# Three quarters of a fused LayerNorm and linear layer by Strassen's seven products, on eight cores

## The chip, the cores and the metric

The kernel runs on the eight cores of one Trainium2 chip. Each core works on 1024 of the 8192 tokens and shares nothing with the others. The metric is the device time of the slowest core in microseconds; lower is better.

## The reference

With `x` of 8192 tokens x 4096 features, `W` of 4096 outputs x 4096 inputs and a bias per output:

```python
def _layernorm(x, axis=-1, eps=1e-5):
    m = jnp.mean(x, axis=axis, keepdims=True)
    v = jnp.var(x, axis=axis, keepdims=True)
    return (x - m) / jnp.sqrt(v + eps)

x = L0_attn_x                                   # (1, 8192, 4096)
x = x + _L0_attn_ref(_layernorm(x))             # softmax over one key: it returns 2 * its input
x = x + _L0_ffn_ref(_layernorm(x), ...)         # y = LN(x) @ (aa * tanh(kk * W)).T + bias
```

The attention has a batch of one, so its softmax is over a single score and is one; its output is twice the normalized input. What is left is two layer norms in a row, which fold into one scale and one offset per token, a large matrix product, and a residual that is again x with one scale and offset per token, plus the bias.

## The kernel before

Each core has 1024 tokens as eight tiles of 128 (`NT`), 4096 inputs as 32 blocks of 128, and 4096 outputs as eight columns of 512 (`NO`). The work has two parts.

In the first part x comes tile by tile. VectorE computes the statistics and from them the coefficients of the token (`statistics`, `coefficients`); ScalarE and GpSimd normalize chunks of 1024 inputs into `h2b` (L384, L242); TensorE transposes them (L424), and ScalarE copies the transposed chunks from PSUM into `h2T` (L391), which holds all 1024 tokens, inputs on the partitions, in bf16. Meanwhile W arrives in pieces of 512 KB (128 inputs x 2 blocks x 512 outputs, f32) in a ring of four buffers `wr`; SP loads piece w as soon as ScalarE has done piece w-4 (`load_w`), and ScalarE writes tanh(kk * W) in bf16 into `wp` (L376). `wp` has two buffers of 16 pieces, one column of 512 outputs each.

The product is made in groups: one group is a token tile and a column of outputs, 32 matmuls (16 pieces, two each) that accumulate in one PSUM bank (L439). The tokens are the stationary operand and W the moving one. The order is written out in `tensor_order()`: column 0 is interleaved with the arrival of tiles, then the first five tiles of column 1 go through together, piece by piece, and from there on the groups follow each other, column by column. `closed` lists the groups in the order in which they end, and `bank_of` and `bank_free` give each a bank and the eviction that it waits for (`NBANK` is six; two banks serve the transposes).

VectorE evicts group i in two instructions (`evict`): L345 makes the residual, rb * s1 + bias, and after a drain L353 adds the PSUM bank to it and writes `outs`. GpSimd serves group i (`serve`): it waits for the eviction, stores `outs` (L262) and loads the residual of group i+4 (L254), all in one queue and in this order. `load_bias` brings the bias of a column, broadcast over the partitions. The last eight groups are stored by SP.

Of the kernel before, what the change touches and what calls it, by code (L numbers as in the profile page):

```python
# [17 lines left out]
D = 4096  # L18
TOK = 1024
NT = TOK // 128  # L20
NO = D // 512
# [5 lines left out]
NBANK = 6  # L27
NRB = 4
# [16 lines left out]
JOIN = [0, 3, 6, 9, 12, 15]  # L45

# [46 lines left out]
def build_nc():  # L93
# [3 lines left out]
    w_h = nc.dram_tensor("wpieces", [NO * PPB * 128, PW], F32, kind="ExternalInput")  # L97
    br_h = nc.dram_tensor("biasrow", [1, D], F32, kind="ExternalInput")
# [3 lines left out]
    y_h = nc.dram_tensor("y", [TOK, D], F32, kind="ExternalOutput")  # L102
# [20 lines left out]
    sc = sb("sc", [128, 8], F32)  # L123

# [6 lines left out]
    acc = [es.enter_context(nc.psum_tensor(f"acc{i}", [128, 512], F32)) for i in range(NBANK)]  # L131
    ptr = [es.enter_context(nc.psum_tensor(f"ptr{i}", [128, CW], BF16)) for i in range(2)]
# [21 lines left out]
    s_ev = sem("s_ev")  # L154

# [13 lines left out]
    NG = len(closed)  # L169

# [19 lines left out]
    @block.sync  # L190
    def _(sync):
        def load_x(t):
            for c in range(NCH):
                if t in before:
                    wait_normalized(sync, before[t], c)
                sync.dma_start(x_of[t][:, c * CW:(c + 1) * CW],  # L196
                               x_h[t * 128:(t + 1) * 128, c * CW:(c + 1) * CW]).then_inc(s_x[t % 4][c], 16)

        def load_w(w):
            if w >= RING:  # L200
                sync.wait_ge(s_wt, w - RING + 1)
# [24 lines left out]
        for i in range(NG - NT, NG):
            t, ot = closed[i]
            sync.wait_ge(s_ev, i + 1)
            sync.dma_start(y_h[t * 128:(t + 1) * 128, ot * 512:(ot + 1) * 512],
                           outs[i % NRB][:, :]).then_inc(s_z[i % NRB], 16)  # L230
        for i in range(NRB):
            sync.wait_ge(s_y[i], 16 * ((NG - NT) // NRB))
            sync.wait_ge(s_z[i], 16 * (NT // NRB))

    @block.gpsimd
    def _(gpsimd):
# [38 lines left out]
        for i in range(EVICTED, NG):  # L275
            serve(i)

    @block.vector
    def _(vector):
# [54 lines left out]
        def evict(i):  # L334
# [110 lines left out]

    es.close()
# [35 lines left out]
```

## Time and profile before

| | us |
|---|---|
| median of 3 runs (lowest to highest) | 522.54 (520.4 to 523.31) |
| the profiled execution, device time | 519.82 |
| its span, slowest core | 518.3 |
| spans of the eight cores | 513.1 to 518.3 |
| mean granted TensorE clock of the cores | 0.965 to 0.979 |

Rows of the trace are of the slowest core, in microseconds from the start of its span. Busy time of an engine is the time in which it executes; its idle time before an instruction is put down to what released it. Matmuls are pipelined, so their busy times overlap, and a few records can be missing; spacings between evictions are the safer clock.

### The profile page before, as it was taken

The numbers are of one execution on the slowest core, as the hardware profiler recorded it, in microseconds if no ns is written. First come the engines' busy times: TensorE is split into PE (matmuls) and PEld (weight loads), VectorE is DVE, ScalarE is ACT, GpSimd is POOL, SyncE is SP. The second block draws the span as 40 slices with busy tenths as digits, with TensorE's granted clock in tenths as the row PEclk, the third lists the DMA queues.
The fourth block names the chain that finished last, engine by engine and source line by source line (L and its number), as shares of the span: only waits on it lengthen the run. The fifth ranks groups of instructions, "written<-read, shape, count | busy, mean of one in ns | idle before, by whom it ended". The sixth has DMA issues, their size and how long they took to land.

```text
span 518.3 us, 6903 instructions; the slowest of 8 cores (513.1 to 518.3 us)
## 1 busy us (share of the span) xinstructions
PE 475.9 (92%) x2364; PEld 225.4 (43%) x2364; DVE 161.1 (31%) x337; ACT 194.8 (38%) x177; POOL 87.3 (17%) x142
## 2 busy tenths in 40 slices
PE   0676879869999999999999999999999999999996
PEld 0543345435444444444444444444444444444442
DVE  1776585883003322222112222221122222211221
ACT  0496756675466244414350324314430435000000
POOL 0111111443003121111111211111111211110000
PEclk9857989989999999999999999999999999999999
DMA  6999999879999999965995399828993696222211
GB/s 169 301 287 316 299 301 272 316 238 264 306 279 255 317 329 330 302 237 165 274 338 218 78 265 291 319 83 249 306 308 132 140 300 270 81 82 81 83 40 41
DMA packets 35282, 120.02 MB, mean 232 GB/s; under 512 B 5168, under 2 KB 5168, under 8 KB 35248
## 3 DMA queue, kind: packets, MB, share of 16 engines
q1 hardware_dynamic: 25056, 87.57, 53.2%
q0 software_dynamic: 9760, 31.99, 20.9%
q8 instruction: 19, 0.31, 0.2%
q14 instruction: 15, 0.12, 0.2%
q10 hardware_dynamic: 432, 0.03, 0.1%
HBM read 102.79 MB, written 16.78 MB: 231 GB/s over the span
## 4 chain that ended last, share of the span: by engine, by line
PE 77%; DMA 12%; DVE 4%; SPq 2%; issue 1%; DVEq 1%; ACT 1%; ACTq 0%
PE acc L439 77%; DMA xs<-x 7%; DMA wr<-wpieces 6%; SPq L196 2%; DVE stats L298 1%; PE ptr L424 1%; ACT h2b L384 0%; ACT wp L376 0%; DVEq L299 0%; SPq L202 0%; DVE sc L288 0%; DVE sc L284 0%; DVEq L347 0%; DVE mv L300 0%; DVE sc L290 0%
## 5 line engine op out<-in xcount | busy, mean ns | idle before, releaser
L439 PE MATMUL acc<-wp,h2T 128*128 128x512 bf16 x2048 | 452.5, 382 | 6.1 <-ACT wp L376 6.0
L439 PEld LDWEIGHTS acc<-wp,h2T 128*128 128x128 bf16 x2048 | 200.2, 98 | 246.2 <-issue 12.5
L376 ACT ACTIVATE wp<-wr,kk_sb 128x1024 bf16<-128x1024 f32 x128 | 144.5, 1146 | 202.1 <-DMA wr<-wpieces 130.8
L353 DVE SCALAR_TENSOR_TENSOR outs<-acc,b1a,rb 128x512 f32<-128x512 f32 x64 | 48.1, 751 | 299.2 <-PE acc L439 296.8
L262 POOL DMA_DIRECT2D y<-outs x56 | 30.7, 548 | 282.7 <-DVE outs L353 282.3
L345 DVE SCALAR_TENSOR_TENSOR rb<-rb,s1a,bb 128x512 f32<-128x512 f32 x64 | 47.6, 744 | 17.1 <-DMA rb<-x 16.6
L424 PE MATMUL ptr<-ident_sb,h2b 128*128 128x128 bf16 x256 | 23.8, 257 | 17.6 <-ACT h2b L384 17.2
L254 POOL DMA_DIRECT2D rb<-x x60 | 32.8, 546 | 27.3 <-DVE outs L353 24.9
L298 DVE BATCH_NORM_STATS2 stats<-xs 128x6 f32<-128x512 f32 x48 | 29.8, 681 | 20.4 <-DMA xs<-x 20.0
L391 ACT COPY h2T<-ptr 128x1024 bf16<-128x1024 bf16 x32 | 31.1, 1011 | 11.9 <-PE ptr L424 11.8
L424 PEld LDWEIGHTS ptr<-ident_sb,h2b 128*128 128x128 bf16 x256 | 20.5, 118 | 27.5 <-issue 25.6
L242 POOL TENSOR_SCALAR h2b<-xs,cf 128x1024 bf16<-128x1024 f32 x12 | 16.2, 1360 | 69.5 <-DVE cf L325 69.5
L413 PE MATMUL acc<-ident_sb 128*128 128x128 bf16 x60 | 5.8, 289 | 14.5 <-DMA aa_sb<-aa 14.5
L384 ACT ACTIVATE h2b<-xs,cf 128x1024 bf16<-128x1024 f32 x12 | 14.2, 1232 | 11.7 <-DVE cf L325 11.7
L413 PEld LDWEIGHTS acc<-ident_sb 128*128 128x128 bf16 x60 | 5.7, 135 | 14.4 <-issue 14.4
L298 DVE BATCH_NORM_STATS2 stats<-h2T 128x6 f32<-128x512 f32 x16 | 10.2, 685 | 4.7 <-DMA h2T<-x 4.5
L242 POOL TENSOR_SCALAR h2b<-h2T,cf 128x1024 bf16<-128x1024 f32 x4 | 4.7, 1195 | 21.1 <-DVE cf L325 21.1
L376 ACT ACT_TABLE_LOAD x1 | 1.3, 1283 | 16.8 <-DMA wr<-wpieces 16.8
L284 DVE TENSOR_SCALAR sc<-sc 128x1 f32<-128x1 f32 x16 | 4.4, 273 | 1.3
L288 DVE TENSOR_SCALAR sc<-sc 128x1 f32<-128x1 f32 x16 | 4.4, 273 | 1.3
L384 ACT ACTIVATE h2b<-h2T,cf 128x1024 bf16<-128x1024 f32 x4 | 4.7, 1226 | 0.0
L248 POOL DMA_DIRECT2D bb<-biasrow x6 | 3.3, 546 | 0.0
(16 smaller groups left out, 22.5 us busy)
## 6 DMA issues: line engine op xcount, KB each, us to landing
wr<-wpieces SPq DMA_DIRECT2D x128, 512.0 KB, 8.8
rb<-x POOLq DMA_DIRECT2D x60, 256.0 KB, 7.2
y<-outs POOLq DMA_DIRECT2D x56, 256.0 KB, 6.0
xs<-x SPq DMA_DIRECT2D x24, 512.0 KB, 13.7
h2T<-x SPq DMA_DIRECT2D x8, 512.0 KB, 18.8
y<-outs SPq DMA_DIRECT2D x8, 256.0 KB, 2.0
bb<-biasrow POOLq DMA_DIRECT2D x6, 256.0 KB, 11.1
rb<-x SPq DMA_DIRECT2D x4, 256.0 KB, 11.4
```

The costliest lines, as they stand in the source:

```text
L242: gpsimd.tensor_scalar(h2b[:, c * CW:(c + 1) * CW], x_of[t][:, c * CW:(c + 1) * CW], cf[t % 2][:, 0:1], cf[t % 2][:, 1:2], ALU.mult, ALU.a ...
L254: gpsimd.dma_start(rb[i % NRB][:, :], x_h[t * 128:(t + 1) * 128, ot * 512:(ot + 1) * 512]).then_inc(s_rb[i % NRB], 16)
L262: gpsimd.dma_start(y_h[t * 128:(t + 1) * 128, ot * 512:(ot + 1) * 512], outs[i % NRB][:, :]).then_inc(s_y[i % NRB], 16)
L298: vector.bn_stats(stats[:, 6 * k:6 * k + 6], x_of[t][:, 512 * k:512 * (k + 1)])
L345: vector.scalar_tensor_tensor(r[:, :], r[:, :], s1a[:, t:t + 1], bb[ot % 2][:, :], ALU.mult, ALU.add)
L353: vector.scalar_tensor_tensor(o[:, :], acc[bank_of[t, ot]][:, :], b1a[:, t:t + 1], r[:, :], ALU.add, ALU.add).then_inc(s_ev, 1)
L376: scalar.activation(wp[ot % 2][:, p * PW:(p + 1) * PW], wr[w % RING][:, :], AF.Tanh, bias=0.0, scale=kk[:, :]).then_inc(s_wt, 1)
L384: scalar.activation(h2b[:, c * CW:(c + 1) * CW], x_of[t][:, c * CW:(c + 1) * CW], AF.Identity, bias=cf[t % 2][:, 1:2], scale=cf[t % 2][:, ...
L391: scalar.copy(h2T[:, t * D + c * CW:t * D + (c + 1) * CW], ptr[c % 2][:, :]).then_inc(s_eA, 1)
L413: tensor.matmul(acc[0][:, 0:128], ident[:, :], ident[:, :], start=True, stop=True)
L424: mm = tensor.transpose(ptr[i % 2][:, q * 128:(q + 1) * 128], h2b[:, c * CW + q * 128:c * CW + (q + 1) * 128], ident[:, :])
L439: mm = tensor.matmul(acc[bank_of[t, ot]][:, :], h2T[:, t * D + k * 128:t * D + (k + 1) * 128], wp[ot % 2][:, k * 512:(k + 1) * 512], start ...
```

## The change

The first 1024 outputs are made as before (`NO` is now 2: 16 groups). The other 3072 are made in 12 pairs (`NP`) of two blocks of 128 outputs by Strassen's method, in which a 2 x 2 block product takes seven block products instead of eight. The halves of A are tokens (512 each) x inputs (2048 each); the halves of B are inputs x the two output blocks of the pair. The result is made transposed: W is now stationary, 128 outputs wide, and the tokens are the moving operand, four tiles of 128 columns at once. A product is 16 matmuls in one bank, and all eight banks take part once the transposes are over.

Sums of quarters of A are made once by VectorE, in bf16, on 128x2048 at a time, four for each of five sums: sA5, sA2 and sA1 in regions that x and `wp` had used, A12-A22 and A21-A11 in place in `h2T`. Sums of W (S6, D12, S7, D21, S1) are made by VectorE for every pair, five adds on 128x2048 in bf16. `B22` has one buffer, the other blocks and sums two. The residual comes transposed from the host (`xt`), two blocks of 128 x 1024 a pair in f32; GpSimd multiplies each by a row of scales and adds a row of offsets (`srow`, `brow`, broadcast over the partitions from a small tensor in DRAM that SP writes and reads back). VectorE then adds each product to its one or two quarters of C with the right sign (`take`), 12 instructions a pair, one with the bias each quarter. SP stores the quarters of C. The host transposes the result of these outputs back.

The diff, cut to its core:

```diff
-NO = D // 512
+NO = 2
+DS = NO * 512
+NP = (D - DS) // 256
+PRODUCTS = ["M5", "M3", "M4", "M2", "M6", "M7", "M1"]
+READS = 12
+LEFT = {"M5": 2, "M3": 4, "M4": 6, "M2": 8, "M6": 9, "M7": 10, "M1": 12}
+BLOCKS = ["B22", "B12", "B11", "B21"]
+SUMS = 5
...
+    pool = [(6, ("tr", 0)), (7, ("tr", 0))] + [(b, ("ev", n)) for b, n in free]
+    for j in range(NP):
+        for m in PRODUCTS:
+            pbank[j, m], pfree[j, m] = pool.pop(0)
+            pool.append((pbank[j, m], ("rd", READS * j + LEFT[m])))
+    A_OF = {"M1": (tiles(sA1), 5), "M2": (tiles(sA2), 2), "M3": (quarter(0, 0), 0), "M4": (quarter(1, 1), 0),
+            "M5": (tiles(sA5), 1), "M6": (quarter(1, 0), 4), "M7": (quarter(0, 1), 3)}
+    B_OF = {"M1": ("S1", "wc", 5), "M2": ("B11", "wt", 6), "M3": ("B12", "wc", 2), "M4": ("B21", "wc", 4),
+            "M5": ("B22", "wt", 2), "M6": ("S6", "wc", 1), "M7": ("S7", "wc", 3)}
...
     def _(sync):
+        def load_xt(j, o):
+            p = j % 2
+            if j == 0:
+                sync.wait_ge(s_tr, NCH * NT)
+            elif j == 1:
+                for i in range(NRB):
+                    sync.wait_ge(s_y[i], 16 * (NG // NRB))
+            else:
+                sync.wait_ge(s_so[p][o], 32 * (j // 2))
+            sync.dma_start(C[p][o], xt_h[256 * j + 128 * o:256 * j + 128 * (o + 1), :]).then_inc(s_xt[p][o], 16)
+        def store(j, i, o, read):
+            sync.wait_ge(s_rd, READS * j + read)
+            sync.dma_start(yt_h[256 * j + 128 * o:256 * j + 128 * (o + 1), 512 * i:512 * (i + 1)],
+                           C[j % 2][o][:, 512 * i:512 * (i + 1)]).then_inc(s_so[j % 2][o], 16)
...
+        for j in range(NP):
+            last = j == NP - 1
+            for i in range(8):
+                if i == 2 and j > 0:
+                    store(j - 1, 0, 0, 11)
+                    store(j - 1, 1, 1, 12)
+                if i == 4:
+                    store(j, 0, 1, 3)
+                if i == 5 and not last:
+                    load_xt(j + 1, 0)
+                    load_xt(j + 1, 1)
+                if i == 6:
+                    store(j, 1, 0, 7)
+                if not last:
+                    load_w(w)
+                    w += 1
...
     def _(gpsimd):
         for i in range(EVICTED, NG):
             serve(i)
+        gpsimd.wait_ge(s_sb, 32)
+        for j in range(NP):
+            for o in (1, 0):
+                c = C[j % 2][o]
+                gpsimd.wait_ge(s_xt[j % 2][o], 16 * (j // 2 + 1))
+                gpsimd.tensor_tensor(c, c, srow, ALU.mult)
+                gpsimd.drain()
+                gpsimd.tensor_tensor(c, c, brow, ALU.add).then_inc(s_bs, 1)
...
     def _(vector):
+        def sums(j, names):
+            p = j % 2
+            for n in names:
+                if n == "S6":
+                    vector.wait_ge(s_wt, W0 + 8 * j + 6)
+                if n == "S7":
+                    vector.wait_ge(s_wt, W0 + 8 * j + 8)
+                if n in ("S6", "S7", "S1") and j >= 2:
+                    vector.wait_ge(s_mm, len(PRODUCTS) * (j - 1))
...
+                vector.tensor_tensor(slot[out, p], slot[a, p], slot[b, p], op).then_inc(s_wc, 1)
+        def take(j, m, ops):
+            vector.wait_ge(s_mm, nth_product[j, m])
+            bank = acc[pbank[j, m]][:, :]
+            for i, o, sign, bias in ops:
+                c = C[j % 2][o][:, 512 * i:512 * (i + 1)]
+                vector.drain()
...
+                    vector.scalar_tensor_tensor(c, bank, float(sign), c, ALU.mult, ALU.add).then_inc(s_rd, 1)
...
-        for i in range(EVICTED, NG):
+        for i in range(EVICTED, 6):
             evict(i)
+        for i in range(4):
+            add_tile(i, tiles(sA5), quarter(0, 0), quarter(0, 1), ALU.add)
+        evict(6)
+        evict(7)
+        for i in range(4):
+            add_tile(i, tiles(sA2), quarter(1, 0), quarter(1, 1), ALU.add)
+        for i in range(8, 8 + EARLY):
+            evict(i)
+        for i in range(4):
+            add_tile(i, quarter(0, 1), quarter(0, 1), quarter(1, 1), ALU.subtract)
+        vector.drain().then_inc(s_sa, 1)
+        sums(0, ["S6", "D12", "S7", "D21"])
+        for i in range(4):
+            if i > 0:
+                evict(8 + EARLY + i - 1)
+            add_tile(i, quarter(1, 0), quarter(1, 0), quarter(0, 0), ALU.subtract)
+        vector.drain().then_inc(s_sa, 1)
+        for j in range(NP):
+            vector.wait_ge(s_bs, 2 * j + 1)
+            take(j, "M5", [(0, 1, 1, False)])
+            vector.wait_ge(s_bs, 2 * j + 2)
+            take(j, "M5", [(0, 0, -1, False)])
+            take(j, "M3", [(0, 1, 1, True), (1, 1, 1, False)])
+            take(j, "M4", [(1, 0, 1, False), (0, 0, 1, False)])
+            take(j, "M2", [(1, 0, 1, True), (1, 1, -1, False)])
+            if j == 0:
+                for i in range(4):
+                    add_tile(i, tiles(sA1), quarter(0, 0), quarter(1, 1), ALU.add)
+                vector.drain().then_inc(s_sa, 1)
+                sums(0, ["S1"])
+            take(j, "M6", [(1, 1, 1, True)])
+            if j + 1 < NP:
...
+                sums(j + 1, ["S6", "D12"])
+            take(j, "M7", [(0, 0, 1, True)])
+            take(j, "M1", [(0, 0, 1, False), (1, 1, 1, False)])
+            if j + 1 < NP:
+                sums(j + 1, ["S7", "D21", "S1"])
...
     def _(scalar):
+        for j in range(NP):
+            for i, b in enumerate(BLOCKS):
+                if b == "B22":
+                    if j == 0:
+                        scalar.wait_ge(s_grp, last_of[0] + 1)
+                    else:
+                        scalar.wait_ge(s_mm, nth_product[j - 1, "M5"])
+                        scalar.wait_ge(s_wc, SUMS * j)
...
+                elif j >= 2:
+                    scalar.wait_ge(s_mm, len(PRODUCTS) * (j - 1))
+                for k in range(2):
+                    scalar.wait_ge(s_w[w % RING], 16 * (w // RING + 1))
+                    scalar.activation(slot[b, j % 2][:, k * PW:(k + 1) * PW], wr[w % RING][:, :],
+                                      AF.Tanh, bias=0.0, scale=kk[:, :]).then_inc(s_wt, 1)
+                    w += 1
...
     def _(tensor):
+        for j in range(NP):
+            for m in PRODUCTS:
+                a, na = A_OF[m]
+                b, what, nb = B_OF[m]
+                if na and j == 0:
+                    tensor.wait_ge(s_sa, na)
+                if what == "wt":
+                    tensor.wait_ge(s_wt, W0 + 8 * j + nb)
+                else:
+                    tensor.wait_ge(s_wc, SUMS * j + nb)
...
+                for k in range(16):
+                    mm = tensor.matmul(acc[pbank[j, m]][:, :], slot[b, j % 2][:, k * 128:(k + 1) * 128],
+                                       a[:, :, k * 128:(k + 1) * 128],
+                                       start=(k == 0), stop=(k == 15))
+                mm.then_inc(s_mm, 1)
```

`s_mm` counts products made, `s_rd` takes, `s_wc` sums of W, `s_wt` tanh pieces, `s_bs` scaled blocks of C, `s_sa` sums of A.

## Rows read from the trace of the kernel before

**Rows 1.** The page: busy time of each engine, and slices of the span.
```profile
PE 475.9 (92%) x2364; PEld 225.4 (43%) x2364; DVE 161.1 (31%) x337; ACT 194.8 (38%) x177; POOL 87.3 (17%) x142
...
GB/s 169 301 287 316 299 301 272 316 238 264 306 279 255 317 329 330 302 237 165 274 338 218 78 265 291 319 83 249 306 308 132 140 300 270 81 82 81 83 40 41
```

**Rows 2.** The page: the chain that ended last, by line.
```profile
PE acc L439 77%; DMA xs<-x 7%; DMA wr<-wpieces 6%; SPq L196 2%; DVE stats L298 1%; PE ptr L424 1%; ACT h2b L384 0%; ACT wp L376 0%; DVEq L299 0%; SPq L202 0%; DVE sc L288 0%; DVE sc L284 0%; DVEq L347 0%; DVE mv L300 0%; DVE sc L290 0%
```

**Rows 3.** Windows: busy time by engine, granted clock, DMA share and rate.
```profile
112.00:119.00 7.00, 6.43 (x37) 4.10 (x38) 5.03 (x7) 4.49 (x5) 6.53 (x10) 0.55 0.72 220
119.00:183.00 64.00, 64.00 (x305) 29.20 (x303) 13.70 (x19) 31.56 (x28) 10.54 (x20) 1.00 0.95 290
183.00:514.00 331.00, 331.00 (x1534) 149.88 (x1532) 67.89 (x97) 91.64 (x81) 49.31 (x92) 1.00 0.65 207
514.00:518.30 4.30, 0.01 (x1) 0.00 (x0) 0.75 (x1) 0.00 (x0) 0.00 (x0) 0.93 0.17 63
```

**Rows 4.** Timeline of VectorE: evictions 16 and 63, each waiting for its group's end.
```profile
189.51 0.75 DVE L353 SCALAR_TENSOR_TENSOR outs<-acc,b1a,rb 128x512 f32<-128x512 f32 x1 [3.23 <-PE acc L439]
...
514.12 0.75 DVE L353 SCALAR_TENSOR_TENSOR outs<-acc,b1a,rb 128x512 f32<-128x512 f32 x1 [5.50 <-PE acc L439]
```

**Rows 5.** Timeline of TensorE, 99 to 115 us: transposes at full clock, and after a gap.
```profile
99.92 0.61 PE L424 MATMUL ptr<-ident_sb,h2b 128*128 128x128 bf16 x8
100.36 1.03 PE L439 MATMUL acc<-wp,h2T 128*128 128x512 bf16 x4
...
112.57 1.01 PE L424 MATMUL ptr<-ident_sb,h2b 128*128 128x128 bf16 x8 [4.68 <-ACT h2b L384]
```

**Rows 6.** Groups of instructions by line and form.
```profile
L353 DVE SCALAR_TENSOR_TENSOR outs<-acc,b1a,rb 128x512 f32<-128x512 f32 x64 | 48.1, 751 | 299.2 <-PE acc L439 296.8 <-issue 2.2
L345 DVE SCALAR_TENSOR_TENSOR rb<-rb,s1a,bb 128x512 f32<-128x512 f32 x64 | 47.6, 744 | 17.1 <-DMA rb<-x 16.6 <-issue 0.5
...
L290 DVE SCALAR_TENSOR_TENSOR sc<-sc 128x1 f32<-128x1 f32 x16 | 2.5, 159 | 1.2
```

**Rows 7.** Timeline of VectorE, 111 to 173 us: evictions 2, 3, 6, 7 and 12.
```profile
111.17 0.75 DVE L345 SCALAR_TENSOR_TENSOR rb<-rb,s1a,bb 128x512 f32<-128x512 f32 x1 [0.24 <-issue]
...
112.75 0.74 DVE L345 SCALAR_TENSOR_TENSOR rb<-rb,s1a,bb 128x512 f32<-128x512 f32 x1
...
121.40 0.75 DVE L345 SCALAR_TENSOR_TENSOR rb<-rb,s1a,bb 128x512 f32<-128x512 f32 x1 [3.72 <-DMA rb<-x]
122.36 0.75 DVE L353 SCALAR_TENSOR_TENSOR outs<-acc,b1a,rb 128x512 f32<-128x512 f32 x1 [0.21 <-issue]
...
160.16 0.75 DVE L353 SCALAR_TENSOR_TENSOR outs<-acc,b1a,rb 128x512 f32<-128x512 f32 x1 [31.40 <-PE acc L439]
...
172.65 0.75 DVE L353 SCALAR_TENSOR_TENSOR outs<-acc,b1a,rb 128x512 f32<-128x512 f32 x1 [0.21 <-issue]
```

**Rows 8.** Timeline of GpSimd: its normalization, alone and beside L345.
```profile
22.14 2.37 POOL L242 TENSOR_SCALAR h2b<-xs,cf 128x1024 bf16<-128x1024 f32 x2 [21.44 <-DVE cf L325]
...
111.18 3.37 POOL L242 TENSOR_SCALAR h2b<-xs,cf 128x1024 bf16<-128x1024 f32 x2 [7.88 <-DVE cf L325]
```

**Rows 9.** DMA issues by line: the whole span, then 175 to 200 and 231 to 287 us.
```profile
rb<-x POOLq DMA_DIRECT2D x60, 256.0 KB, 7.2
...
wr<-wpieces SPq DMA_DIRECT2D x8, 512.0 KB, 9.6
...
wr<-wpieces SPq DMA_DIRECT2D x16, 512.0 KB, 6.5
```

**Rows 10.** Timeline of ScalarE behind a stop of the W stream, 345 to 366 us.
```profile
348.41 4.27 ACT L376 ACTIVATE wp<-wr,kk_sb 128x1024 bf16<-128x1024 f32 x4 [16.16 <-PE acc L439]
354.08 1.15 ACT L376 ACTIVATE wp<-wr,kk_sb 128x1024 bf16<-128x1024 f32 x1 [1.41 <-DMA wr<-wpieces]
360.79 2.37 ACT L376 ACTIVATE wp<-wr,kk_sb 128x1024 bf16<-128x1024 f32 x2 [5.56 <-DMA wr<-wpieces]
365.29 1.15 ACT L376 ACTIVATE wp<-wr,kk_sb 128x1024 bf16<-128x1024 f32 x1 [2.13 <-DMA wr<-wpieces]
```

More of the change, by code:

```diff
@@ L109, in build_nc, with part @@
     h2T = sb("h2T", [128, NT * D], BF16)
-    wp = [sb(f"wp{i}", [128, PPB * PW], BF16) for i in range(2)]
-    xs = [sb(f"xs{i}", [128, D], F32) for i in range(2)]
-    h2b = sb("h2b", [128, D], BF16)
     wr = [sb(f"wr{i}", [128, PW], F32) for i in range(RING)]
-    rb = [sb(f"rb{i}", [128, 512], F32) for i in range(NRB)]
-    outs = [sb(f"outs{i}", [128, 512], F32) for i in range(NRB)]
-    bb = [sb(f"bb{i}", [128, 512], F32) for i in range(2)]
+    early = sb("early", [128, 36 * 1024], BF16)
+    late = sb("late", [128, 26 * 1024], BF16)
+    def part(region, kb, size, dt=BF16):
+        v = region[:, kb * 512:(kb + size) * 512]
+        return v.bitcast(F32) if dt == F32 else v
+    xs = [part(early, 0, 16, F32), part(early, 16, 16, F32)]
+    h2b = part(early, 32, 8)
+    wp = [part(early, 40, 32), part(late, 0, 32)]
+    rb = [part(late, 32 + 2 * i, 2, F32) for i in range(NRB)]
+    outs = [part(late, 40 + 2 * i, 2, F32) for i in range(NRB)]
+    bb = [part(late, 48 + 2 * i, 2, F32) for i in range(2)]
+    sA5, sA2, sA1 = part(early, 0, 16), part(early, 16, 16), part(late, 0, 16)
+    C = [[part(early, 32 + 4 * o, 4, F32) for o in range(2)], [part(late, 44 + 4 * o, 4, F32) for o in range(2)]]
+    srow, brow = part(early, 40, 4, F32), part(early, 44, 4, F32)
+    slot = {}
+    for i, n in enumerate(["B12", "B11", "B21", "S6", "S7"]):
+        slot[n, 0], slot[n, 1] = part(early, 52 + 4 * i, 4), part(late, 20 + 4 * i, 4)
+    slot["S1", 0], slot["S1", 1] = part(late, 16, 4), part(late, 40, 4)
+    slot["B22", 0] = slot["B22", 1] = part(early, 48, 4)
     kk = sb("kk_sb", [128, 1], F32)
@@ L154, in build_nc @@
     s_ev = sem("s_ev")
+    s_rows = sem("s_rows")
+    s_sb = sem("s_sb")
+    s_bc = sem("s_bc")
+    s_xt = [[sem(f"s_xt{p}{o}") for o in range(2)] for p in range(2)]
+    s_so = [[sem(f"s_so{p}{o}") for o in range(2)] for p in range(2)]
+    s_bs = sem("s_bs")
+    s_sa = sem("s_sa")
+    s_wc = sem("s_wc")
+    s_mm = sem("s_mm")
+    s_rd = sem("s_rd")
     todo = tensor_order()
@@ L221, in _ @@
                     w += 1
-        while w < NO * PPB:
+        while w < W0:
             load_w(w)
             w += 1
[L226 to L230, printed above, removed]
+        sync.wait_ge(s_cf, NT)
+        for i, v in enumerate((s1a, b1a)):
+            sync.dma_start(bass.AP(rows_h, i * TOK, [[1, 128], [128, NT]]), v[:, :],
+                           allow_slow_non_contiguous=True).then_inc(s_rows, 16)
@@ new lines, in _ @@
+        for _ in range(4):
+            load_w(w)
+            w += 1
[13 more added lines that the diff above has]
+                if not last:
+                    load_w(w)
+                    w += 1
@@ L231, in _ @@
+        store(NP - 1, 0, 0, 11)
+        store(NP - 1, 1, 1, 12)
         for i in range(NRB):
-            sync.wait_ge(s_y[i], 16 * ((NG - NT) // NRB))
-            sync.wait_ge(s_z[i], 16 * (NT // NRB))
+            sync.wait_ge(s_y[i], 16 * (NG // NRB))
+        for p in range(2):
+            for o in range(2):
+                sync.wait_ge(s_so[p][o], 32 * (NP // 2))
     @block.gpsimd
@@ new lines, in take @@
+        def take(j, m, ops):
[3 more added lines that the diff above has]
+                c = C[j % 2][o][:, 512 * i:512 * (i + 1)]
+                vector.drain()
+                if bias:
+                    vector.scalar_tensor_tensor(c, bank, bcol[:, 2 * j + o:2 * j + o + 1], c,
+                                                ALU.add, ALU.add).then_inc(s_rd, 1)
+                else:
+                    vector.scalar_tensor_tensor(c, bank, float(sign), c, ALU.mult, ALU.add).then_inc(s_rd, 1)
@@ new lines, in _ @@
+        for c in range(NCH):
+            wait_normalized(vector, 7, c)
+        wait_transposed(vector, 7, NCH - 1)
+        for i in range(4):
[7 more added lines that the diff above has]
+        sums(0, ["S6", "D12", "S7", "D21"])
```

99 lines of the change are left out of this document (70 added, 29 removed).

## The prediction

> **What bounds the kernel now.** I read the page first: TensorE is busy 92% of the span, VectorE 31%, ScalarE 38%, with HBM traffic mostly at 230 to 330 GB/s until it fades at the end [rows 1]. The chain that ended last gives 77% to matmul line L439; nothing else holds over 7%, and all of that lies early [rows 2]. The windows then split the span: up to 119 us TensorE waits for x, W and normalization, from 119 to 514 us it never idles at a granted clock of 1.00, and 4.3 us of eviction and store close it [rows 3]. So the kernel is TensorE-bound where the change acts. Its pace is read from evictions that wait for PE: 47 groups between 189.51 and 514.12 us [rows 4], so 6.907 us for the 32 matmuls of a group, 0.2158 us for one. The eviction at 189.51 us is that of the 17th group, so the 16th closes at about 182.4 us; the last closes near 513.9.
>
> **What goes and what comes.** The first 16 groups (outputs 0 to 1023) stay as they are, so everything up to 182.4 us is nearly unchanged. Behind it stood 48 groups x 6.907 = 331.5 us. In their place come 12 pairs x 7 products x 16 matmuls = 1344 matmuls of the same 128x128 by 128x512 shape, 3.453 us a product, 24.17 a pair, 290.1 in all: 41.4 us less. The moving operand is now four runs of 128 columns; back-to-back 128-column transposes start 0.44 us per eight at full clock [rows 5], so four cost 0.22 us, and 2% is the most that I allow for it; I take nothing.
>
> **Durations of the new work.** VectorE: a `take` has the form of the PSUM eviction, 0.751 us [rows 6], and with the drain ahead of it I take 0.96, the spacing from L345 to L353 [rows 7]. A two-input bf16 add over 2048 elements is in no row. The f32 form costs 744 ns for 512 elements and 159 ns for one [rows 6], so 1.145 ns an element: 2.50 us if the new add goes by elements, 1.33 if by bytes. I take 1.33, a choice, since both inputs and the output are two bytes wide; 2.50 stays as a rival. The Trainium skill (VectorE: DVE Perf Modes, the perf-mode tier table) says that a bf16 tensor_tensor yields two results a cycle and gives 1224 ns for 2048 elements; by it the whole sum below would be 498.8 instead of 503.2 (20 adds in the start, 0.106 less each, and a ring under 24.17). No row here shows it.
> GpSimd scales C with two-input f32 operations on 1024 elements. With one input two of them took 2.37 us, 1.19 each [rows 8]; one to two times that are the bounds, and I take 2.4, 9.6 us a pair. ScalarE: 8 tanh pieces x 1.15 = 9.2 us a pair [rows 10], off the path. DMA: 4 MB of W, 1 of xT and 1 of yT, 6.3 MB per 24.2 us or 260 GB/s, below the 290 GB/s that the stretch 119 to 183 sustained [rows 3].
>
> **The start of the products.** VectorE must evict groups 8 to 12 before it may overwrite tiles. In the trace eviction 12 starts at 172.65, for its residual came late behind W traffic [rows 7]; its issue was near 162. W traffic now ends sooner (8 pieces, not a stream), so with the median landing of 7.2 us [rows 9] and 1.7 of eviction I put its end at 170.4 (bounds 168 and 173.4). The first matrix sums, sA5 and sA2, fall into VectorE's idle stretches (117.7 to 121.4 and 128 to 160) and cost nothing; without that cover they would add 10.6 us. Then comes one serial chain: four subtracts 5.3 (175.7); S6, D12, S7, D21 5.5 (181.2); three subtracts and evictions 13 to 15, 4.0 + 3 x 1.62 (190.1). GpSimd's queue is the trap: its scaling of C stands behind `serve(15)`, so it begins at 191.2 and ends at 200.8. VectorE cannot take product M5 before; eight takes and sA1 and S1 follow: 201.8, 207.5, 212.8, 214.2. TensorE needs S1 for M1, the seventh product, due at 182.4 + 6 x 3.453 = 203.1. It waits 11.1 us.
> A second wait follows from it. B22 has one buffer and S1 reads it, so ScalarE's pair-1 tanh starts at 214.2, and only then is the ring slot free for piece 4: W, two xT, W, 2 MB. The 2 MB of a full ring took 6.5 to 9.6 us [rows 9]; I take 9.5. Then tanh (226.1), S6 and D12 (228.9); M3 of pair 1, ready at 221.1, waits 7.8. S7 and D21 come at 234.5, M4 waits 2.1 more. Both gaps lower the clock: a 4.68 us gap is followed by transposes of 1.01 instead of 0.61 us a batch [rows 5], and the clock is 0.55 over that window [rows 3], near the lower of its two levels, about 2.5 us lost. Most of it falls into the next wait; I add 0.5. Sum of the start: 21.5 us.
>
> **The steady pair.** Three paces compete. TensorE: 24.17. VectorE: 12 x 0.96 + 5 x 1.33 + 0.4 = 18.6. The third is a ring through four queues. SP waits for the first take of M3 (rd 3) before it stores and issues W piece 4, both xT and piece 5; S6 of the next pair needs piece 5; VectorE works in order. Landing of 2.25 MB (a store, two W pieces, two xT) 10.4 us: after an idle time the first 0.5 MB landed 4.5 us after its issue (tanh 348.41 + 1.15 to 354.08 [rows 10]), and the other 1.75 MB (1.84 million bytes) take 5.9 at 310 GB/s, between the 290 of the stretch [rows 3] and the best slices [rows 1]. Then tanh 1.3, S6 and D12 2.8, three takes 2.9, S7, D21, S1 4.1, two takes of M5 and the one of M3 2.9: 24.4 us. So the ring is as long as TensorE's pair and a little more; I take 24.4 for ten pairs, +2.3 us. Banks do not bind: a bank comes back eight products later. The GpSimd side of the ring, xT landed at 8, scaling 9.6 to 12, two takes, is 22 at most.
> The tail has one more take, +1.0.
>
> **Sum.** 519.8 (the profiled execution; its span is 518.3) - 41.4 + 21.5 + 2.3 + 1.0 = 503.2. The median of the runs shown is 522.5, 0.5% above the profiled one, so 506 for the median.
>
> **Rivals.**
> (A, forecast, 0.43) as above, 498 to 511.
> (B) the ring binds: same mechanism, longer landing. Each us of landing over 10.4 costs 10 us. The restart of [rows 10] speaks for it: its second piece came some 10 us after issue, and the fourth at 365.3, 15.7 us after the first was issued. Against it: that restart also carried a bias broadcast, which is gone now. At 11 to 11.8 us: 512 to 520 (0.22). It decides at a pair of 26.0 us, a landing of 12.0 us: from there on the kernel is slower than before. At 13 us the time is 532 (0.08). This is the other side.
> (C, 0.05) the adds go by elements: the ring grows by 5 x 1.17 to 30.2 us and the start, with 20 adds in its chain, by some 23 us: 587. With 1.57 us an add the gain is gone.
> (D, 0.08) VectorE and GpSimd shut each other out: S6 and D12 each wait for a scaling, some 3.5 us a pair: 541. The one overlap in the trace speaks against it: two f32 two-input adds kept 0.75 us while GpSimd's pair took 3.37 instead of 2.37 us [rows 7, 8]; GpSimd pays, not VectorE. The Trainium skill (SBUF — State Buffer, who interferes with whom) says that a VectorE instruction with two SBUF inputs contends with GpSimd's reads, and that who comes first holds the ports for the whole instruction. By that rule D would come out; the row bears it out for GpSimd's side alone.
> (E, 0.14) the start is cheaper: eviction 12 by 168, scaling nearer 1.2 us an operation (5 us less in the chain), a ring below 24.17: 488 to 497.
>
> **The numbers.** A difference under 0.5% (2.6 us) is about what measuring cannot tell from none. Faster: A, E and B up to 519.9, 0.78. Within 0.5%: 0.03. Slower: the rest of B, C and D, 0.19. The range 488 to 526 leaves out C, D and the long part of B, under 0.2; A's own is 498 to 511.
>
> **What would show it.** In the new profile: 1856 matmuls with bf16 operands; the product of pair 0 that waits longest is M1, with VectorE's S1 as releaser, about 11 us, at 203 us; a second gap of some 8 us in front of M3 of pair 1, with VectorE's D12; GpSimd's first scaling near 191 us, 2.4 us each; adds of 1.33 us; from pair 2 on no TensorE idle time and 24.2 to 24.4 us a pair. Wrong would make it: adds above 1.6 us, W pieces landing over 12 us after their issue in the steady part, gaps before M3 or M4 in every pair, or a clock below full in the steady part.

## The result and the profile after

The changed kernel takes 554.3 us (median of 4 runs, 553.3 to 555.0; a fifth took 558.6) against 521.8 for the kernel before (520.4 to 523.3): 1.065 times the time, 95% interval 1.059 to 1.071. The forecast was 506, range 488 to 526, faster. It is slower by 32.5 us, and 48 us above the forecast.

The page of the changed kernel, slowest core (4 of 8). In the profiled execution, as in a few of the experiments' runs, one die's cores had a lower clock and were longer (here by 2.5%), so the ratios and the medians of the experiments leave such executions out, and core 0 of the other die is read beside core 4.

```profile
span 551.7 us, 6892 instructions; the slowest of 8 cores (524.1 to 551.7 us)
...
PE 443.6 (80%) x2157; PEld 207.0 (38%) x2172; DVE 333.5 (60%) x465; ACT 194.0 (35%) x177; POOL 170.8 (31%) x96
...
GB/s 187 292 290 312 332 296 297 171 259 294 126 39 293 286 193 39 20 218 204 253 151 293 206 239 174 264 198 299 178 310 145 308 153 314 192 263 213 250 59 57
...
DMA 34%; PE 22%; DVE 16%; DVEq 9%; SPq 8%; issue 5%; ACT 4%; POOLq 1%; POOL 1%; ACTq 0%
```

Against [rows 1] TensorE has 32 us less work and is busy 80% of a longer span. The chain that ended last, 77% TensorE in [rows 2], is now 22%: a ring of DMA, VectorE and the queues. The forecast saving was 41.4; what is missing went into matmuls at a lower clock behind the gaps, and all that was saved and 33 us more into waits. Two slices with 126 and 39 GB/s stand at 138 to 165 us, where [rows 3] has 290 on average.

TensorE's timeline, core 4. In brackets is its idle time and who ended it; L684 is the products' line; x16 is one product, x32 are two in a row:

```profile
183.01 3.62 PE L684 MATMUL acc<-early 128*128 128x512 bf16 x16
198.07 9.63 PE L684 MATMUL acc<-h2T,early 128*128 128x512 bf16 x32 [11.44 <-DVE early L499]
...
233.87 5.35 PE L684 MATMUL acc<-late 128*128 128x512 bf16 x16 [15.81 <-DVE late L499]
239.06 3.62 PE L684 MATMUL acc<-early 128*128 128x512 bf16 x16
254.73 8.62 PE L684 MATMUL acc<-h2T,late 128*128 128x512 bf16 x32 [12.06 <-DVE late L499]
...
283.90 8.75 PE L684 MATMUL acc<-h2T,early 128*128 128x512 bf16 x32 [3.29 <-DVE early L499]
...
339.37 3.61 PE L684 MATMUL acc<-h2T,early 128*128 128x512 bf16 x16 [0.50 <-DVE early L499]
344.25 3.61 PE L684 MATMUL acc<-h2T,early 128*128 128x512 bf16 x16 [1.27 <-DVE early L499]
...
448.35 3.61 PE L684 MATMUL acc<-h2T,early 128*128 128x512 bf16 x16 [1.27 <-DVE early L499]
```

The products begin at 183.0, as forecast (182.4). Then M3 of pair 0 waits 11.4 us (forecast none), M1 15.8 (forecast 11.1), M3 of pair 1 12.1 (forecast 7.8). From pair 4 to pair 8 M3 starts at 339.37 and 448.35: 27.2 us a pair, where 24.2 is TensorE's own. From pair 2 to the last (M3 at 283.9 and 526.7) it is 27.0, on core 0 25.7 (269.34 and 500.92). Pairs are counted from 0; on core 4 each of pairs 0 to 9 has a gap in front of M3 or M4, on core 0 each of all twelve, a sign that the prediction named as one that would prove it wrong.

How the steady pair is made, core 4, one turn of VectorE's timeline (L499 are sums of W, L509 and L512 takes), and ahead of it two sums of the pair before:

```profile
305.08 1.23 DVE L499 TENSOR_TENSOR late<-late 128x2048 bf16<-128x2048 bf16 x1 [4.60 <-ACT late L627]
306.40 3.20 DVE L499 TENSOR_TENSOR late<-late,early 128x2048 bf16<-128x2048 bf16 x1
...
332.46 6.66 DVE L499 TENSOR_TENSOR early<-early 128x2048 bf16<-128x2048 bf16 x2 [3.03 <-ACT early L627]
339.22 0.75 DVE L509 SCALAR_TENSOR_TENSOR late<-acc,bcol,late 128x512 f32<-128x512 f32 x1
340.07 1.48 DVE L512 SCALAR_TENSOR_TENSOR late<-acc,late 128x512 f32<-128x512 f32 x2
341.47 2.53 DVE L499 TENSOR_TENSOR early<-early 128x2048 bf16<-128x2048 bf16 x2
343.92 1.22 DVE L499 TENSOR_TENSOR late<-early 128x2048 bf16<-128x2048 bf16 x1
345.23 1.48 DVE L512 SCALAR_TENSOR_TENSOR early<-acc,early 128x512 f32<-128x512 f32 x2
346.80 0.75 DVE L509 SCALAR_TENSOR_TENSOR early<-acc,bcol,early 128x512 f32<-128x512 f32 x1
```

GpSimd's timeline over the same stretches (from 329.90 on each pair of lines is one half of xT, times s1 and plus b1):

```profile
305.37 3.15 POOL L395 TENSOR_TENSOR late<-late,early 128x1024 f32<-128x1024 f32 x1
...
329.90 2.35 POOL L393 TENSOR_TENSOR early<-early 128x1024 f32<-128x1024 f32 x1 [14.53 <-DMA early<-xt]
332.40 2.34 POOL L395 TENSOR_TENSOR early<-early 128x1024 f32<-128x1024 f32 x1
334.70 3.33 POOL L393 TENSOR_TENSOR early<-early 128x1024 f32<-128x1024 f32 x1
338.17 3.15 POOL L395 TENSOR_TENSOR early<-early 128x1024 f32<-128x1024 f32 x1
```

S6 and D12 take 6.66 us while GpSimd scales, S7 and D21 2.53 when it is idle. Who starts first decides who pays: the sum at 305.08 began before GpSimd's operation of 305.37 and kept 1.23 us, while that operation went from 2.35 to 3.15; the sum at 306.40 found it under way and took 3.20. Over all eight cores the 28 sums that began just ahead of an operation kept 1.21 to 1.23 us, and of the 182 that began while one was under way 136 took 3.2 us or more, 3.42 at most. The takes (one PSUM input) beside the same scaling keep 0.69 and 0.75 us.

The ring of the forecast is there link by link: the take of M3 ends at 320.0, SP's store, two W pieces and two xT follow, ScalarE has piece 5 done at 332.3 (12.3 us; forecast 11.7), S6 and D12 6.7 (forecast 2.8), three takes 2.3, three sums 3.8, three takes 2.4, and the next take of M3 ends at 347.6: 27.5 us against the 24.4 forecast.

The start, core 4, SP's queue (the number behind the start is the stretch that the group covers):

```profile
140.50 0.45 SPq L298 DMA_DIRECT2D rows<-s1a  x1
141.00 0.64 SPq L298 DMA_DIRECT2D rows<-b1a  x1
141.69 11.52 SPq L300 DMA_DIRECT2D bcol<-biascol  x1
153.31 9.55 SPq L272 DMA_DIRECT2D wr<-wpieces  x4
162.96 2.15 SPq L311 DMA_DIRECT2D early<-xt  x2
```

and DMA issues between 130 and 200 us, with the median time to landing:

```profile
wr<-wpieces SPq DMA_DIRECT2D x16, 512.0 KB, 13.4
...
rows<-s1a SPq DMA_DIRECT2D x1, 4.0 KB, 19.1
rows<-b1a SPq DMA_DIRECT2D x1, 4.0 KB, 22.7
```

Two transfers of 4 KB, 1024 runs of 4 bytes each, take 19.1 and 22.7 us (13.2 and 13.5 on core 0). SP needs 11.5 us to get the next one out, a load of 12 KB in 128 runs that lands after 22.4, and the rate over 140 to 160 us is 61 GB/s on this core (96 on core 0, against 291 in the kernel before). With the stores gone (the second experiment) that load leaves SP in 0.4 us and lands in 4.9. The W pieces of pair 0 come late; VectorE, done with its subtractions at 182.8, waits 12.4 us for them.

### The profile page after: what moved, and what is told of

Same layout as the page of the kernel before. It is cut to its first block, busy times and chain, and to the rows that moved or that the text cites. A ratio compares the mean times of both kernels' runs of the same rounds, so it can differ in the third digit from the quotient of the medians.

```text
span 551.7 us, 6892 instructions; the slowest of 8 cores (524.1 to 551.7 us)
## 1 busy us (share of the span) xinstructions
PE 443.6 (80%) x2157; PEld 207.0 (38%) x2172; DVE 333.5 (60%) x465; ACT 194.0 (35%) x177; POOL 170.8 (31%) x96
## 4 chain that ended last, share of the span: by engine, by line
DMA 34%; PE 22%; DVE 16%; DVEq 9%; SPq 8%; issue 5%; ACT 4%; POOLq 1%; POOL 1%; ACTq 0%
DMA wr<-wpieces 27%; PE acc L684 21%; DMA early<-x 7%; DVEq L507 6%; DVE early L499 5%; DVE late L499 4%; SPq L300 2%; SPq L272 2%; SPq L266 2%; ACT early L627 1%; SPq L311 1%; DVE stats L417 1%; DVEq L463 1%; ACT late L578 1%; POOLq L394 1%
## 5 line engine op out<-in xcount | busy, mean ns | idle before, releaser
L627 ACT ACTIVATE early<-wr,kk_sb 128x1024 bf16<-128x1024 f32 x60 | 66.9, 1145 | 199.1 <-DVE late L499 123.2
L684 PE MATMUL acc<-h2T,late 128*128 128x512 bf16 x384 | 89.6, 392 | 25.0 <-DVE late L499 25.0
L684 PE MATMUL acc<-h2T,early 128*128 128x512 bf16 x384 | 89.6, 392 | 20.8 <-DVE early L499 20.8
L499 DVE TENSOR_TENSOR early<-early 128x2048 bf16<-128x2048 bf16 x24 | 50.0, 2088 | 29.0 <-ACT early L627 27.9
L661 PE MATMUL acc<-early,h2T 128*128 128x512 bf16 x246 | 62.5, 397 | 6.0 <-ACT early L578 5.2
L684 PEld LDWEIGHTS acc<-h2T,late 128*128 128x128 bf16 x384 | 37.9, 100 | 75.2 <-issue 34.3
L684 PE MATMUL acc<-early 128*128 128x512 bf16 x288 | 65.1, 379 | 0.0
L684 PEld LDWEIGHTS acc<-h2T,early 128*128 128x128 bf16 x384 | 38.0, 100 | 71.2 <-issue 30.1
L627 ACT ACTIVATE late<-wr,kk_sb 128x1024 bf16<-128x1024 f32 x36 | 41.1, 1147 | 55.3 <-DMA wr<-wpieces 54.8
L684 PE MATMUL acc<-late 128*128 128x512 bf16 x192 | 45.1, 390 | 15.8 <-DVE late L499 15.8
L661 PE MATMUL acc<-late,h2T 128*128 128x512 bf16 x251 | 55.2, 379 | 0.3
L499 DVE TENSOR_TENSOR late<-late 128x2048 bf16<-128x2048 bf16 x12 | 25.6, 2131 | 34.4 <-ACT late L627 33.8
L512 DVE SCALAR_TENSOR_TENSOR early<-acc,early 128x512 f32<-128x512 f32 x48 | 33.2, 692 | 16.6 <-POOL early L395 11.8
L684 PEld LDWEIGHTS acc<-early 128*128 128x128 bf16 x288 | 28.2, 98 | 34.0
L512 DVE SCALAR_TENSOR_TENSOR late<-acc,late 128x512 f32<-128x512 f32 x48 | 33.2, 692 | 8.8 <-PE acc L684 4.6
L661 PEld LDWEIGHTS acc<-early,h2T 128*128 128x128 bf16 x256 | 24.9, 102 | 32.5 <-issue 9.6
## 6 DMA issues: line engine op xcount, KB each, us to landing
wr<-wpieces SPq DMA_DIRECT2D x128, 512.0 KB, 8.2
early<-x SPq DMA_DIRECT2D x24, 512.0 KB, 15.7
early<-xt SPq DMA_DIRECT2D x12, 512.0 KB, 6.9
late<-xt SPq DMA_DIRECT2D x12, 512.0 KB, 7.8
h2T<-x SPq DMA_DIRECT2D x8, 512.0 KB, 19.3
```

Of the source, the lines that this page charges most:

```text
L499: vector.tensor_tensor(slot[out, p], slot[a, p], slot[b, p], op).then_inc(s_wc, 1)
L512: vector.scalar_tensor_tensor(c, bank, float(sign), c, ALU.mult, ALU.add).then_inc(s_rd, 1)
L627: scalar.activation(slot[b, j % 2][:, k * PW:(k + 1) * PW], wr[w % RING][:, :], AF.Tanh, bias=0.0, scale=kk[:, :]).then_inc(s_wt, 1)
L661: mm = tensor.matmul(acc[bank_of[t, ot]][:, :], h2T[:, t * D + k * 128:t * D + (k + 1) * 128], wp[ot % 2][:, k * 512:(k + 1) * 512], start ...
L684: mm = tensor.matmul(acc[pbank[j, m]][:, :], slot[b, j % 2][:, k * 128:(k + 1) * 128], a[:, :, k * 128:(k + 1) * 128], start=(k == 0), sto ...
```

## The experiments

Each ran beside the kernel before, whose median beside them was 520.3 to 522.8 us; times are medians, and the gains are against 554.3.

**Two causes, one at a time and together.** The first edit takes GpSimd's scaling out:

```diff
-        for j in range(NP):
-            for o in (1, 0):
...
-                gpsimd.tensor_tensor(c, c, srow, ALU.mult)
-                gpsimd.drain()
-                gpsimd.tensor_tensor(c, c, brow, ALU.add).then_inc(s_bs, 1)
...
-            vector.wait_ge(s_bs, 2 * j + 1)
+            vector.wait_ge(s_xt[j % 2][1], 16 * (j // 2 + 1))
```

> The changed kernel without GpSimd's scaling of C (the residual of the transposed outputs goes in unscaled and without its offset); VectorE waits for xT itself. All transfers stay. Theory 1, VectorE's adds and GpSimd's scaling slow each other (an add takes 3.2 us beside a scaling and 1.22 alone; S6 and D12 together 6.7 instead of 2.5): all adds go at 1.22, the ring falls from 27 to about 23.5, so TensorE sets the pair at 24.2, 10 pairs x 2.5 = 25 to 28 us less, and the start is shorter by the 9.7 to 12 us of scaling ahead of the first take: 515 to 520 in all. Theory 2, the landing of W pieces alone makes the ring long and the slow adds are hidden: only the start gets shorter, pairs stay at 26 to 27, 543 in all.

Measured 507.2 us, 47 less, ratio to the kernel before 0.976 (0.971 to 0.981). The group of VectorE's adds in its profile, by shape (count, then busy time and mean ns of one, then the idle time ahead of them):

```profile
L491 DVE TENSOR_TENSOR early<-early 128x2048 bf16<-128x2048 bf16 x24 | 29.3, 1223 | 21.3 <-ACT early L619 20.2
```

TensorE's timeline of the same kernel, with its last gaps:

```profile
189.52 8.60 PE L676 MATMUL acc<-h2T,early 128*128 128x512 bf16 x32 [7.03 <-DVE early L491]
214.37 6.36 PE L676 MATMUL acc<-late 128*128 128x512 bf16 x16 [5.73 <-DVE late L491]
232.32 9.38 PE L676 MATMUL acc<-h2T,late 128*128 128x512 bf16 x32 [8.13 <-DVE late L491]
```

All adds take 1.22 us, and no gap follows 232 us: TensorE sets the pair. Theory 2 falls. The gain is above the 34 to 39 expected, since the start got more: its three waits fell from 39.3 to 20.9 us. M3 of pair 2, 49 us behind TensorE's own pace in the changed kernel, is 28 behind here (258.80, where 178.87 + 15 x 3.453 = 230.7): 21 us, where 9.7 to 12 had been put.

The second takes out the stores of the rows:

```diff
-        for i, v in enumerate((s1a, b1a)):
-            sync.dma_start(bass.AP(rows_h, i * TOK, [[1, 128], [128, NT]]), v[:, :],
-                           allow_slow_non_contiguous=True).then_inc(s_rows, 16)
...
-            sync.dma_start(v, bass.AP(rows_h, i * TOK, [[0, 128], [1, TOK]])).then_inc(s_sb, 16)
+            sync.dma_start(v, bass.AP(x_h, i * D, [[0, 128], [1, TOK]])).then_inc(s_sb, 16)
```

> The changed kernel without the two stores of s1 and b1 as rows in DRAM (2048 runs of 4 bytes); the two broadcast loads stay but read x, so that scales and offsets are not the right numbers. Theory 1, these stores and what queues behind them hold the DMA engines from 140 to 160 us (27 to 96 GB/s where 290 stood before): the stretch goes back to 280 to 300 GB/s, the eight W pieces of pair 0 are ready before VectorE asks for them (its wait of 5 to 12 us before the first S6 vanishes), the residual of group 12 comes up to 4 us earlier, and the kernel is 10 to 16 us faster, about 540. Theory 2, the stretch is low because SP has nothing to load while it waits for ring slots: no change beyond 2 us.

Measured 535.5 (3 runs), 19 less. The windows 140 to 160 and 160 to 180 us carry 238 and 329 GB/s, the wait in front of M3 of pair 0 is gone, and M1 of pair 0 still waits 14.1 us. The steady part is as slow as it was: M3 of pair 2 at 261.45, of pair 11 at 507.54, 27.3 us a pair. The gain is above the 10 to 16 expected.

> Both edits: no scaling on GpSimd and no stores of the rows. If the two causes are separate, the gains add: about 38 to 44 us less than the changed kernel, 510 to 516, with pairs of 24.2 us, no gap in front of M3 of pair 0, and what is left of the start the order of VectorE's sums: M1 of pair 0 waits some 4 to 6 us, and M3 of pair 1 some 8 for the chain through B22. If they overlap, the sum is 5 us or more short of the two gains.

Measured 492.6, 62 less; 47 and 19 are 66, so the two are nearly separate. It is 17 us below the expected range: scaling costs more in the start than I had put, and the range was less than the two expected gains together (34 to 39 and 10 to 16). Of the waits in front of M1 of pair 0 and M3 of pair 1, 4.8 and 7.0 us are left.

**The ring, cut in SP's queue.**

```diff
-                if i == 4:
-                    store(j, 0, 1, 3)
-                if i == 5 and not last:
+                if i == 4 and not last:
                     load_xt(j + 1, 0)
                     load_xt(j + 1, 1)
                 if i == 6:
-                    store(j, 1, 0, 7)
+                    store(j, 0, 1, 3)
                 if not last:
                     load_w(w)
                     w += 1
+            store(j, 1, 0, 7)
```

> The changed kernel with SP's order alone changed, outputs as the reference: both xT of the next pair go out ahead of W piece 4, and the two stores that wait for takes of M3 and M2 go behind pieces 5 and 7, so no load waits for a take. Theory 1, the ring through the take of M3 is the bound of the pair, with the slowed adds inside it: cut here, pieces 5 and 7 land some 4 us earlier, adds and scaling still overlap but have time to spare, pairs fall to 24.2 to 24.8 us: 525 to 530. xT of pair 1 also comes before S1, which takes up to 5 us off the second wait of the start. Rival, VectorE's own work with slowed adds is the bound: pairs stay above 26 and only 2 to 6 us are won.

Measured 517.9 (10 runs), 36 less, 0.994 of the kernel before (0.991 to 0.998), and 7 us better than the range expected. VectorE's timeline in its profile, two adds beside the scaling:

```profile
339.47 1.99 DVE L498 TENSOR_TENSOR late<-late 128x2048 bf16<-128x2048 bf16 x1
341.55 3.20 DVE L498 TENSOR_TENSOR late<-late,early 128x2048 bf16<-128x2048 bf16 x1
```

and TensorE's, with its last gaps:

```profile
234.51 5.84 PE L683 MATMUL acc<-late 128*128 128x512 bf16 x16 [18.55 <-DVE late L498]
247.23 9.76 PE L683 MATMUL acc<-h2T,late 128*128 128x512 bf16 x32 [3.42 <-DVE late L498]
298.85 3.61 PE L683 MATMUL acc<-h2T,late 128*128 128x512 bf16 x16 [0.20 <-DVE late L498]
303.74 3.61 PE L683 MATMUL acc<-h2T,late 128*128 128x512 bf16 x16 [1.27 <-DVE late L498]
```

The adds beside the scaling are as slow as before, 3.20 us here, but S6 no longer waits for its piece behind a take, and TensorE has no gap after 304 us. So neither the slow adds nor the ring alone is the bound: the slow adds cost time because they stand in a ring that was as long as TensorE's pair already.

**The rows made on the chip**, with the stores replaced by matmuls that spread s1 and b1 over the partitions, each as the sum of two bf16 halves, and by copies out of PSUM on VectorE: two vectors, eight tiles, two halves, so 32 matmuls (the expectation counted 64).

```diff
...
+                for r in range(NT):
+                    for part_ in range(2):
+                        k = 16 * i + 8 * part_ + r
+                        mm = tensor.matmul(acc[6 + r // 4][:, (r % 4) * 128:(r % 4 + 1) * 128],
+                                           hl[:, k:k + 1].to_broadcast([128, 128]), ident[:, :],
+                                           start=(part_ == 0), stop=(part_ == 1))
...
```

> The changed kernel with the rows of scales and offsets made on the chip instead of through DRAM: TensorE multiplies s1 and b1 (as two bf16 halves, spread over 128 columns) with the identity, 64 matmuls of 128 columns into the two transpose banks, VectorE copies them out. Outputs as the reference. Nothing else moves. Theory: the small stores cost what their removal gave (18 us with the stores gone), and the detour costs TensorE some 4 us: 538 to 542, and the DMA rate from 140 to 160 us is again near 290 GB/s. Rival, the gain came from the missing dependence on the rows: 550.

Measured 536.0 (3 runs), 18 less, with 291 GB/s in 140 to 160 us. The stores were the cost, and no dependence on the rows.

**VectorE's order at the start**, with SP's new order:

```diff
+        for i in range(4):
+            add_tile(i, tiles(sA1), quarter(0, 0), quarter(1, 1), ALU.add)
+        vector.drain().then_inc(s_sa, 1)
+        sums(0, ["S1"])
         vector.wait_ge(s_bc, 16)
...
-            if j == 0:
...
-                sums(0, ["S1"])
```

> The changed SP order of the earlier run, and VectorE's sA1 and S1 for pair 0 moved ahead of the takes of pair 0, so that M1 of pair 0 and the tanh of pair 1 no longer wait for GpSimd's scaling. Outputs as the reference. Theory: in the run with SP's order alone M1 waited 18.6 us and M3 of pair 1 3.4 more; S1 would be ready some 6 us after the last eviction, so the wait falls to 2 to 6 us and the kernel is 14 to 18 us faster than with SP's order alone: 500 to 504. Rival, the takes that now come 6 us later fill the banks or hold the ring back: 512 to 518.

Measured 508.0 (3 runs, 505.5 to 512.0), 10 less than with SP's order alone, where 14 to 18 were expected. M1 of pair 0 waits 5.0 us instead of 18.6, but here the rows' stores cost 15.9 us in front of M3 of pair 0 (11.5 in the other profile), and M3 of pair 1 still waits 5.0. The place of the wait was right, the size was not.

**All four edits**: SP's order, the rows on the chip, VectorE's order at the start, and as the fourth an earlier start (scaling of pair 0 ahead of the service of group 8, the subtractions ahead of eviction 12, xT of pair 0 ahead of its W):

> Outputs as the reference; four edits together: SP's order, rows on TensorE, sA1 and S1 ahead of the takes, and an earlier start (scaling of pair 0 ahead of the service of group 8, subtractions and sums ahead of eviction 12, xT of pair 0 ahead of W of pair 0). If the start is only these waits, TensorE has no gap over 2 us behind 119 us, pairs of 24.2, plus 4 us for the rows: 482 to 490. If something unseen is next (banks, W pieces for column 1 later by the xT load), 495 to 505.

Measured 483.4 us (4 runs, 482.6 to 484.3), 0.926 of the kernel before (0.924 to 0.929) and 71 us below the change as it was made. Busy time of the engines in its profile:

```profile
PE 433.7 (90%) x2204; PEld 206.9 (43%) x2204; DVE 324.4 (67%) x473; ACT 194.7 (40%) x177; POOL 162.8 (34%) x96
```

and its windows, the start and the pairs behind it (start and end, the time between, then for PE, PEld, DVE, ACT, POOL the busy time with the instructions; the last three are granted clock, DMA share and GB/s):

```profile
119.00:187.00 68.00, 68.00 (x353) 32.27 (x351) 40.13 (x46) 24.61 (x23) 21.11 (x26) 1.00 0.81 256
187.00:477.00 290.00, 289.23 (x1339) 130.66 (x1337) 205.21 (x206) 99.26 (x88) 118.42 (x46) 1.00 0.70 236
```

Behind 119 us TensorE has two gaps in all, 0.41 and 0.32 us, at full granted clock. The gain of 39 us over the kernel before (522.0 us beside it) is most of the 41.4 that the fewer matmuls should give.

**The ring with the start repaired**: the same kernel with SP's order set back.

> The best kernel so far (all four edits, 483.9 us) with SP's order set back to that of the change: the stores that wait for takes stand again ahead of xT and W piece 5. Outputs as the reference. Theory, with the start repaired what is left of the loss is the ring, 2 to 3 us a pair over 11 pairs: 506 to 517. Rival, the ring bound only because the start had left VectorE behind: 484 to 492.

Measured 515.6, 32 us more than with the new order, 0.988 of the kernel before (0.982 to 0.994). M3 goes from 268.31 to 486.21 in eight pairs, 27.2 us each. The ring needs no bad start.

**What GpSimd must do to slow an add.** Two kernels keep the old queues and change only its work on C. In the first, four one-input operations stand in place of the two with two inputs:

```diff
-                gpsimd.tensor_tensor(c, c, srow, ALU.mult)
+                gpsimd.tensor_scalar(c, c, 1.5, 0.25, ALU.mult, ALU.add)
+                gpsimd.drain()
+                gpsimd.tensor_scalar(c, c, 0.5, 0.125, ALU.mult, ALU.add)
...
```

> The changed kernel with each of GpSimd's two-input operations on C replaced by two one-input ones with constants (the residual goes in wrongly scaled), so GpSimd works about as long but streams one input. Theory 1, any GpSimd read of SBUF slows VectorE's two-input adds: adds beside it take again about 3 us or more. Theory 2, only GpSimd's second input stream takes the port: adds fall to 1.2 to 1.6 us, and the pair to 24.5 to 25.

In the second, two fills stand there:

```diff
-                gpsimd.tensor_tensor(c, c, srow, ALU.mult)
+                gpsimd.memset(c, 1.0)
...
```

> The changed kernel with each of GpSimd's two operations on a block of C replaced by a fill with a constant (the residual of the transposed outputs is lost), so GpSimd writes SBUF and reads nothing. Theory, it is GpSimd's reads that slow VectorE's two-input adds: adds beside a fill take 1.22 us, and the pair is near 24.2, 508 to 520 in all. Rival, any GpSimd work on SBUF slows them: adds of 2 us or more beside a fill.

Beside one-input operations (1.05 us alone) an add takes mostly 1.83 to 1.88 us, 2.11 at most; one such add in VectorE's timeline of the first kernel:

```profile
353.80 1.88 DVE L503 TENSOR_TENSOR late<-late,early 128x2048 bf16<-128x2048 bf16 x1
```

Beside fills (0.95 us) it takes 1.22, as the group of all adds by shape of the second kernel shows:

```profile
L499 DVE TENSOR_TENSOR early<-early 128x2048 bf16<-128x2048 bf16 x24 | 29.4, 1223 | 20.9 <-ACT early L627 17.2 <-PE acc L684 2.6
```

Neither theory of the first has its number: the adds are above the 1.2 to 1.6 us of theory 2 and well below the 3 of theory 1, and a pair takes 25.6 us (542.7 us for that kernel, one run). Theory 1 holds in a weaker form: a read with one input by GpSimd slows the adds too, by less than one of its operations lasts. With fills the time is 520.8 (one run), 0.8 above the range expected, and no gap follows 247 us. Its two longest cores, 519.2 and 513.3 us, were granted 0.81 of the clock from 120 to 180 us in unbroken matmuls; the other six took 499.3 to 510.8 us. The fills are also shorter than the scaling, so that kernel alone does not tell what reading costs from what length does; the duration of the adds does.

## Why the prediction was wrong

The sum was 519.8 - 41.4 + 21.5 + 2.3 + 1.0 = 503.2 against 553.3 of the profiled execution. Up to M3 of pair 2 the core that set the time lost 49 us (283.9, where 183.0 + 15 x 3.453 = 234.8 is TensorE's own), 27.6 more than the 21.5; from there 9 pairs of 27.0 instead of 24.4 are 23.2 more. Together 51, against a miss of 50. Of the 49, 42.6 are four gaps (11.4, 15.8, 12.1, 3.3) and the rest mostly matmuls at a lower clock behind them: the two products at 198.07 took 9.63 us instead of 7.07, at a granted clock of 0.72. The sum had 0.5 for that. Core 0 lost 37.6 us in the start and has pairs of 25.7: the same two places, smaller.

- *The matmuls.* Right: 16 matmuls take 3.45 us with four runs of 128 columns, no 2% lost, and 39 of the 41.4 us show in the repaired kernel.
- *"adds of 1.33 us", rival C.* Right where GpSimd is idle: 1.22 us, which is the 1224 ns of the Trainium skill (VectorE: DVE Perf Modes, the perf-mode tier table). C fell.
- *Rival D, put at 0.08 with "GpSimd pays, not VectorE".* **This step failed.** D came, near its price: 3.5 us a pair were named, and S6 and D12 take 3.9 us more than planned (6.7 for 2.8); the pair came to 27.0 for 24.4. I had argued it away from [rows 7, 8], where the adds kept 0.75 us. There L345 starts at 111.17 and 112.75, GpSimd's operations at 111.18 and 112.9: VectorE came first both times, by 0.01 and 0.15 us. The next L345, at 114.30, began before GpSimd's operation had ended and took 0.79 us: 0.05 more, the only sign of VectorE's side there. In the steady pair GpSimd is mostly first (182 sums against 28), since xT lands ahead of piece 5. The Trainium skill (SBUF — State Buffer, who interferes with whom) says just this, that who comes first holds the ports for the whole instruction; the trace agrees: one add and one scaling side by side advance every 3.5 us (334.70 to 338.17), the sum of 1.22 and 2.35. So it was there too who came first, and the rows did not speak against the rule as I had read them.
- *The ring, rival B.* Its length without that was nearly right (landing and tanh 12.3 for 11.7, takes and the other sums 8.5 for 9.9; with 2.8 for S6 and D12 23.6 for 24.4), so the condition of B, a longer landing, did not come. That it stood within 1% of TensorE's pair should have told me that any of its links, D's above all, costs ten times. I priced B and D as if they could not meet.
- *The stores of the rows.* **A term put at nothing without a reason.** The section on the change names the small tensor that SP writes; I saw a transfer of 4 KB and costed nothing. Each took 13 to 23 us to land, and together they took 18 to 19 us of the kernel.
- *The start.* The two waits, their places, releasers and causes (GpSimd's queue behind `serve(15)`, B22 and S1) were right. Eviction 12 ended at 178.3, not 170.4, on this core: its residual came 4.9 us later than in the kernel before, behind the stores. Without them (the second experiment) it ended at 171.9, scaling began at 190.98 (forecast 191.2) and the two waits were 14.1 and 10.7 us (11.1 and 7.8): most of what the start missed was the stores. The scaling (2.35 for 2.4 us) was right; it had one pause of 2.4 us behind its first operation, for which the trace names no cause.

## What to carry to other kernels

Where a rebalanced pipeline leaves TensorE as the bound, add up every ring that goes through the queues: one that comes within a few per cent of TensorE's period is a second bound, and any slowdown of a link is then paid once a turn. A load should stand ahead of a store that waits for a result, in a queue that serves both; that one change was worth 32 to 36 us here. Price a transfer by its runs and not by its bytes alone, and when an overlap in a trace seems harmless, look who started first.

## What the runs showed of the hardware

- A two-input bf16 add of 128x2048 on VectorE takes 1.22 us alone and also when it begins ahead of GpSimd's operation; begun behind a two-input operation of GpSimd it mostly takes 3.2 (3.42 at most), behind a one-input one 1.88 (2.11 at most), beside a fill 1.23. The scaling itself goes from 2.35 to 3.43 at most. Takes, with one input from PSUM, are not slowed.
- Two stores of 1024 runs of 4 bytes were 19.1 and 22.7 us in landing on one core, 13.2 and 13.5 on another, and pulled a core's rate from 291 to 61 and 96 GB/s over 20 us. No run has the same bytes in longer runs.
- The spans of the cores spread with the waits: 524 to 552 us in the changed kernel, 474.6 to 481.0 in the repaired one, 513 to 518 before. The slowest core sets the time. Why one core has 25.7 and another 27.0 us a pair was not tried.
